# A fused attention block and gated network in float32: the weight sums of the second inner layer are formed and checked in the block runs, behind a third flag

## The chip, the core and the metric

One NeuronCore of a Trainium2 chip runs the whole program in one launch. Its engines are TensorE (PE, with the weight loads shown as PEld), VectorE (DVE), ScalarE (ACT) and GpSimd (POOL); SyncE (SP) issues all transfers, and its queue shows as SPq. The metric is the device time in microseconds.

## The reference

With `xn` the layer-normed input (2 batches of 2048 tokens, 256 channels), the output is `x + attn(xn) + ffn(xn)`, all in float32.

```python
def _L0_ffn_ref(x, w1_w, w1_s, w2_w, w2_s, h1_w, h1_s, h2_w, h2_s, w3_w, w3_s):
    h = silu(_tlin(x, w1_w, w1_s)) * _tlin(x, w2_w, w2_s)      # 256 -> 1024
    h = gelu(_tlin(h, h1_w, h1_s))                             # 1024 -> 1024, "first inner layer"
    h = gelu(_tlin(h, h2_w, h2_s))                             # 1024 -> 1024, "second inner layer"
    return _tlin(h, w3_w, w3_s)                                # 1024 -> 256
# _tlin(x, w, s) = einsum('bsi,oi->bso', x, w) * s, and the weights w are drawn from -1, 0, 1
```

`attn` is a linear attention block: convolutions over tokens, projections, q and k through elu, a 16-head product, a gate, an output projection, a third convolution, a norm and an MLP (256 to 1024 to 256 with gelu).

## The kernel before, in words

The 4096 tokens are 8 tiles of 512. Operands in float32 are split into a high part (type fp32r, whose low 12 bits are taken as zero) and the rest, so that a product is two or three fast matmuls. A weight of -1, 0 or 1 has nothing in its low part, so two matmuls do for the network. That this holds is not assumed: every weight piece, and every sum of pieces, is ORed with the mask 0xFFF into an accumulator (`check`), the accumulator is reduced (`bits`), summed over the partitions by a small matmul (`sum_bits`), written as a flag (`set_flag`), and TensorE loads the flag and branches to a variant of its program with wide or with fast matmuls.

**First half** (`P1_STEPS`): the attention's front, with the network's first layers for tiles 0 to 3 between. **Second half** (`E_STEPS`, -3 to 7): step i runs the output projection of tile i + 2, the MLP of tile i, the norm of tile i + 1 and the attention's rest of tile i + 3. These are the MLP's steps. In the text, step i begins with the output projection of tile i + 2; steps 6 and 7 have none and begin with fc1. Its order on VectorE: y_out(i - 1), x1_out(i + 2), the low parts of the gelus (`h_lo`, L1661) mixed with conv taps (L1424), moments (L1393), attention_out, add_lepe, checks, `pe_lo`, `pm_lo`, more checks. On GpSimd: halo, late sums (or, in step 0, at its end), inverse deviation, the gate (L922), `bias_residual` (L927). `pe_lo` and `pe_hi` are what the output projection of the next step reads.

**Block runs.** For the inner layers a tile is not multiplied by the whole weight directly: the 1024 x 1024 weight is cut into 2 x 2 quarters A11, A12, A21, A22 and the tile into B11 ... B22, and seven products (`PRODUCTS`) of sums of quarters take the place of eight. The weight sums S1 to S4 (`W_SUMS`) of both inner layers are formed on GpSimd, a slice of 128 rows at a time (`late_sums`, u = 0 to 7; u below 4 is the first inner layer, the others the second), in the MLP's steps: SP loads two pieces (`load_late`), GpSimd makes four sums of 128x512, VectorE checks the two halves of the result (and for the second inner layer the two raw pieces), SP saves them to DRAM (`save_sums`, s_s). Later SP loads each product's weights from w_s or s_s (`load_block`).

There are 12 runs of blocks. The first four, t = 0 to 3, each do the network's first layer for tile 4 + t (`first_layer`, on VectorE `gate_up`, on ScalarE `silu_gate`) and then the seven products of the first inner layer; the last eight do the second inner layer, one tile each, and the down projection (`down`). VectorE forms the inputs' sums (`combine`) and low parts (`low_part`, L1778) and adds the products (`sums_to_u2`, `sums_to_u4`, `result_22`, `result_12`, `result_21`). Each engine's order is written out by hand; everything is ordered by counting semaphores (`s_sum`: sums formed, `checked`: checks done, `bits_max`, `flag_set`, `prod`, `u_lo`), and all of an engine's waits are in program order, so an instruction behind a wait waits too. TensorE's second flag is set in step 7 and followed by the branch that holds all twelve runs (L2314 is the branch of the first flag, L2323 that of the second).

## Time and profile before

| | us |
|---|---|
| median of 3 runs | 1128.58 (1125.61 to 1132.94) |
| the profiled execution, whole | 1131.99 |
| its span in the trace | 1130.1 |
| busy: PE / PEld / DVE / ACT / POOL | 1043.5 (92%) / 920.2 (81%) / 769.4 (68%) / 592.7 (52%) / 279.8 (25%) |
| mean granted TensorE clock | 0.976 of full speed |

The profiled execution is one of its own, so a sum made from its rows is set against 1131.99 us, and then moved to the median. In its trace the steps of the second half that the change touches lie between about 425 and 682 us, the four runs with a first layer between 682 and 848, and the other eight behind.

### The profile page before, as it was taken

How to read it: one execution, taken by the hardware profiler on the slowest of the kernel's cores; microseconds unless marked ns; L12 is line 12 of the kernel's file. 1: busy time of each engine (PE TensorE's matmuls, PEld its weight loads, DVE VectorE, ACT ScalarE, POOL GpSimd, SP SyncE). 2: the span in 40 equal slices, each digit the busy share in tenths (PEclk: the TensorE clock that was granted, in tenths of full speed). 3: DMA queues.
4: the chain of work that ended last, by engine and by line, in shares of the span. 5: the costliest groups of instructions: out<-in, count | busy, mean ns of one | idle time of the engine just before them, and what ended most of it. 6: DMA issues, size and time to landing. Idle time of an engine off the chain costs nothing. (4 is left out here: it accounts for less than half of the span.)

```text
span 1130.1 us, 17148 instructions
## 1 busy us (share of the span) xinstructions
PE 1043.5 (92%) x6630; PEld 920.2 (81%) x6630; DVE 769.4 (68%) x948; ACT 592.7 (52%) x853; POOL 279.8 (25%) x231
## 2 busy tenths in 40 slices
PE   3579989999989999899998999999999999999998
PEld 2457877788867678577787878998999989999997
DVE  6586567644645647789988866466576888776764
ACT  3346776566634335444554544456456556554453
POOL 3144335331423323353444520000000110011100
PEclk9799989899999999899999999999999999999999
DMA  8767963554495455144443266121176322332310
GB/s 334 283 224 252 347 239 131 181 164 159 141 357 196 121 196 185 60 149 168 162 147 120 94 243 242 57 72 60 56 266 257 112 77 79 108 104 84 113 38 20
DMA packets 68339, 180.70 MB, mean 160 GB/s; under 512 B 4976, under 2 KB 26096, under 8 KB 64624
## 3 DMA queue, kind: packets, MB, share of 16 engines
q1 hardware_dynamic: 68256, 179.56, 45.7%
q8 instruction: 57, 0.93, 0.3%
q14 instruction: 26, 0.21, 0.1%
HBM read 121.86 MB, written 66.06 MB: 166 GB/s over the span
## 5 line engine op out<-in xcount | busy, mean ns | idle before, releaser
L2025 PE MATMUL pr<-xp_hi,wb 128*128 128x256 f32 x1344 | 320.0, 282 | 2.7 <-DVE p1s L1794 1.8
L2025 PE MATMUL pr<-xp_lo,wb 128*128 128x256 f32 x1344 | 319.5, 282 | 0.0
L2025 PEld LDWEIGHTS pr<-xp_hi,wb 128*128 128x128 f32 x1344 | 255.3, 190 | 4.6 <-issue 4.6
L2025 PEld LDWEIGHTS pr<-xp_lo,wb 128*128 128x128 f32 x1344 | 256.4, 191 | 0.0
L2025 PE MATMUL pr<-u_hi,ring 128*128 128x512 f32 x256 | 103.1, 403 | 2.3 <-issue 1.3
L2025 PE MATMUL pr<-u_lo,ring 128*128 128x512 f32 x256 | 100.7, 394 | 0.0
L983 POOL TENSOR_TENSOR ot<-ot,yg 128x512 f32<-128x512 f32 x14 | 25.2, 1802 | 277.0 <-DVE ot L1815 277.0
L1299 ACT CAST xp_hi<-tf 128x1024 fp32r<-128x1024 f32 x48 | 50.2, 1046 | 52.6 <-PE pr L2025 18.2
L2192 PE MATMUL pr<-wf_hi,h_hi 128*128 128x256 f32 x256 | 75.8, 296 | 0.0
L2192 PE MATMUL pr<-wf_lo,h_hi 128*128 128x256 f32 x256 | 73.0, 285 | 0.0
L2192 PE MATMUL pr<-wf_hi,h_lo 128*128 128x256 f32 x256 | 72.6, 284 | 0.0
L1778 DVE TENSOR_TENSOR xp_lo<-tf,xp_hi 128x1024 fp32r<-128x1024 f32 x48 | 59.1, 1231 | 19.9 <-ACT xp_hi L1299 19.8
L1239 ACT ACTIVATE hf<-pr,fb 128x512 f32<-128x512 f32 x64 | 44.1, 690 | 54.0 <-PE pr L190 40.1
L1661 DVE TENSOR_TENSOR h_lo<-hf,h_hi 128x512 fp32r<-128x512 f32 x64 | 51.7, 818 | 24.5 <-ACT h_hi L1239 24.5
L2025 PE MATMUL pr<-xg_hi,ring 128*128 128x512 f32 x128 | 54.4, 425 | 9.5 <-issue 4.9
L2025 PE MATMUL pr<-wd,a_hi 128*128 128x256 f32 x256 | 60.9, 281 | 2.1 <-DVE a_lo L1808 2.0
L2025 PEld LDWEIGHTS pr<-u_hi,ring 128*128 128x128 f32 x256 | 48.6, 190 | 15.5 <-issue 3.7
L2025 PE MATMUL pr<-wd,a_lo 128*128 128x256 f32 x256 | 60.5, 279 | 0.0
L869 POOL TENSOR_TENSOR u_lo<-full,u_hi 128x512 fp32r<-128x512 f32 x32 | 43.7, 1370 | 61.7 <-DVE u_hi L1531 61.7
L874 POOL TENSOR_TENSOR xg_lo<-xg_lo,xg_hi 128x1024 fp32r<-128x1024 f32 x8 | 20.6, 2574 | 155.2 <-ACT xg_hi L1095 155.2
L2025 PEld LDWEIGHTS pr<-u_lo,ring 128*128 128x128 f32 x256 | 48.6, 190 | 10.3 <-issue 0.5
L1315 ACT ACTIVATE u<-u,prm 128x256 f32<-128x256 f32 x96 | 41.0, 498 | 30.3 <-DVE u L1799 15.2
(219 smaller groups left out, 2623.9 us busy)
## 6 DMA issues: line engine op xcount, KB each, us to landing
ring<-w_s SPq DMA_DIRECT2D x42, 512.0 KB, 5.0
uf<-h_s SPq DMA_DIRECT2D x16, 1024.0 KB, 6.0
late_raw<-w_gated SPq DMA_DIRECT2D x16, 512.0 KB, 5.3
s_s<-late_sum SPq DMA_DIRECT2D x8, 1024.0 KB, 6.6
wb<-s_s SPq DMA_DIRECT2D x8, 1024.0 KB, 8.6
stage<-w_gated SPq DMA_DIRECT2D x4, 1536.0 KB, 10.5
wb<-w_s SPq DMA_DIRECT2D x6, 1024.0 KB, 10.2
vw<-v_s SPq DMA_DIRECT2D x8, 514.0 KB, 7.4
```

Source lines behind the costliest of these rows:

```text
L869: pool.tensor_tensor(u1_lo[:, m, :], full1[:, m % 2, :], u1_hi[:, m, :].bitcast(F32), ALU.subtract) \
L874: pool.tensor_tensor(x_lo[:], xf, x_hi[:].bitcast(F32), ALU.subtract).then_inc(s["x_split"], 1)
L983: pool.tensor_tensor(ot[:, part, :], ot[:, part, :], yg[:, part, :], ALU.add).then_inc(s["out_sum"], 1)
L1239: last = e.activation(out_, F1[:, m % 2, :], ACT.Gelu, bias=fb[:, m:m + 1])
L1299: e.copy(xp_hi[p][:], sources[p]).then_inc(s["u_hi"], 1)
L1315: last = e.activation(results[k][:, m, :], source[:, m, :], ACT.Gelu, scale=par(scale, RESULTS[k][0] * HB + m))
L1661: e.tensor_tensor(h_lo[:, m, :], hf[:, m % 2, :], h_hi[:, m, :].bitcast(F32), ALU.subtract) \
L1778: e.tensor_tensor(xp_lo[p][:], sources[p], xp_hi[p][:].bitcast(F32), ALU.subtract).then_inc(s["u_lo"], 1)
L2025: return e.matmul(bank, w.bitcast(dt), v_.bitcast(dt), start=first, stop=last, skip_group_check=True)
L2192: last = e.matmul(as_tokens(F2)[:, n, :], h[:, k, cols], w[:, k, :], start=(k == 0 and j == 0), stop=(k == KH - 1 and j == 2))
```

## The change

The second inner layer's sums (old u = 4 to 7) leave the MLP's steps. What stays there is spread over steps 1, 2, 4 and 5, one slice each with two checks; the two checks of the down weights go to steps 0 and 3, ahead of `pe_lo`; the bits are reduced in step 5. `bias_residual` moves on GpSimd from behind the gate to the head of the step, behind the halo and ahead of the sums.

In each of block runs 0 to 3, one slice of the second inner layer is now treated in a new buffer, late2, in the place where the down weights lie: SP loads two pieces, VectorE checks them behind gate_up 1 and 3 (into a new accumulator, acc3), GpSimd forms the four sums in place behind these two checks and the low part of xg, VectorE checks them ahead of sums_to_u2 and behind the last `low_part`, SP saves them. In run 3 the accumulator is reduced, and the bits are summed on TensorE ahead of the last product. The second flag now stands for the first inner layer and the down weights; the second branch holds runs 0 to 3, and a third flag with its own branch holds the other eight. On SP the down weights load behind the second layer's blocks, load_xg comes behind save_sums2 and save_result(t - 1, 3), and some loads around load_block(1, ...) change places. The matmuls are the same ones, and 16 checks of VectorE and 16 additions of GpSimd move from the steps to the runs; one reduction, one memset, two small sets of bit sums and one branch are added.

```diff
-LATE = tuple((layer, m) for layer in range(2) for m in range(HB))
-LATE_LOADS = {(0, "first"): (0, 1), (1, "first"): (2,), (2, "first"): (3,), (3, "first"): (4,), (4, "first"): (5,),
-              (5, "first"): (6,), (6, "first"): (7,)}
-LATE_SUMS = {(0, "last"): (0,), **{(i, "first"): (i,) for i in range(1, 8)}}
-LATE_CHECKS = {1: (0, 1), **{i: (i,) for i in range(2, 8)}}
-def checks_of(u):
-    return ["sums"] * 2 + ["raw"] * 2 * LATE[u][0]
+LATE_LOADS = {0: (0, 1), 3: (2,), 4: (3,)}
+LATE_SUMS = {1: 0, 2: 1, 4: 2, 5: 3}
+LAST_CHECKS = (0, 3)
+IN_PLACE = ("S2", "S4", "S3", "S1")
 def checks_before(u):
-    return 1 + sum(len(checks_of(n)) for n in range(u)) + (u >= 3)
+    return 1 + 2 * u + (u >= 2)
+LATE_CHECKS = 2 + 2 * HB
+RUN_CHECKS = 4
...
+        late2 = place("late2", [P, 2, PIECE], RG + 69632)
+        acc3 = place("acc3", [P, PIECE], wo_at, I32)
...
         def sums_kept(e):
             for i in range(2):
-                e.wait_ge(s_kept[i], s_kept_before[i] + 16 * HB)
+                e.wait_ge(s_kept[i], s_kept_before[i] + 16 * (HB // 2))
+        def sums2_kept(e, count):
+            e.wait_ge(s_kept[0], s_kept_before[0] + 16 * (HB // 2 + count))
...
+            def load_late2(n):
+                if n == 0:
+                    sp.wait_ge(s["bits_max"], 2)
+                else:
+                    sums2_kept(sp, n)
+                    sp.wait_ge(s["checked"], STREAM + 3 + LATE_CHECKS + RUN_CHECKS * n)
+                for i in range(2):
+                    sp.dma_start(late2[:, i, :], w_gated[KH // 2 + KH + n + i * HB]).then_inc(late_in[0], 16)
+            def save_sums2(n):
+                sp.wait_ge(s["s_sum"], len(W_SUMS) * (HB + n + 1))
+                sp.dma_start(s_s[HB + n], late2[:].rearrange("p a (b n) -> p (a b) n", b=2)).then_inc(s_kept[0], 16)
...
-                for place in ("first", "last"):
-                    for u in LATE_SUMS.get((i, place), ()):
-                        save_sums(u)
-                for u in LATE_LOADS.get((i, "last"), ()):
-                    load_late(u)
+                if i in LATE_SUMS:
+                    save_sums(LATE_SUMS[i])
                 if i == E_STEPS[-1]:
+                    load_late2(0)
                     load_block(0, 1)
                     load_block(0, 2)
...
             save_y(TILES - 1)
-            sp.wait_ge(s["bits_max"], 2)
-            for i in range(2):
-                sp.dma_start(wd_[:, i, :].bitcast(F32), w_s[STREAM + KH + i]).then_inc(s["wd_in"], 16)
             for t_ in range(BLOCK_RUNS - 1):
-                load_xg(FRONTED + t_ + 1, xg2)
                 if t_ > 0:
                     save_result(t_ - 1, 3)
+                save_sums2(t_)
+                load_xg(FRONTED + t_ + 1, xg2)
                 for k in range(3):
                     save_result(t_, k)
+                load_late2(t_ + 1)
+            save_sums2(BLOCK_RUNS - 1)
             load_block(1, 0)
+            load_block(1, 1)
             save_result(BLOCK_RUNS - 2, 3)
-            load_block(1, 1)
             load_h(0, 0)
+            load_h(0, 1)
             load_block(1, 2)
-            load_h(0, 1)
             for k in range(len(RESULTS)):
                 save_result(BLOCK_RUNS - 1, k)
                 load_block(1, 3 + k)
+            sp.wait_ge(s["bits_max"], 3)
+            for i in range(2):
+                sp.dma_start(wd_[:, i, :].bitcast(F32), w_s[STREAM + KH + i]).then_inc(s["wd_in"], 16)
...
+            def late_sums2(n):
+                pool.wait_ge(s["checked"], STREAM + 3 + LATE_CHECKS + RUN_CHECKS * n + 2)
+                a11, a12, a21, a22 = (late2[:, i // 2, i % 2 * TOK:(i % 2 + 1) * TOK] for i in range(4))
+                before = len(W_SUMS) * (HB + n)
+                pool.tensor_tensor(a22, a21, a22, ALU.add).then_inc(s["s_sum"], 1)
+                pool.tensor_tensor(a21, a11, a21, ALU.subtract).then_inc(s["s_sum"], 1)
+                pool.wait_ge(s["s_sum"], before + 1)
+                pool.tensor_tensor(a11, a22, a11, ALU.subtract).then_inc(s["s_sum"], 1)
+                pool.wait_ge(s["s_sum"], before + 3)
+                pool.tensor_tensor(a12, a12, a11, ALU.subtract).then_inc(s["s_sum"], 1)
...
+                if i >= 0 and valid(i + 2):
+                    bias_residual(i + 2)
                 if i == 0:
                     pool.wait_ge(s["h1_mm"], KH * FRONTED)
                     pool.wait_ge(s["checked"], STREAM + 1)
                     pool.memset(acc2[:], 0).then_inc(s["checked"], 1)
-                for u in LATE_SUMS.get((i, "first"), ()):
-                    late_sums(u)
+                if i in LATE_SUMS:
+                    late_sums(LATE_SUMS[i])
...
-                if valid(i + 1) and valid(i + 2):
-                    bias_residual(i + 2)
-                for u in LATE_SUMS.get((i, "last"), ()):
-                    late_sums(u)
+                if i == -1:
+                    bias_residual(1)
                 front("e", i, "after_back")
-            for j in range(FRONTED, TILES):
-                low_of_xg(j, xg2_lo, xg2, xg2_hi)
+            pool.wait_ge(s["g_prod"], TILES)
+            pool.wait_ge(s["checked"], STREAM + 2 + LATE_CHECKS)
+            pool.memset(acc3[:], 0).then_inc(s["checked"], 1)
+            for n in range(BLOCK_RUNS):
+                low_of_xg(FRONTED + n, xg2_lo, xg2, xg2_hi)
+                late_sums2(n)
...
+            def check_late(u, n):
+                e.wait_ge(s["s_sum"], len(W_SUMS) * (u + 1))
+                sums = late_sum[u % 2][:].rearrange("p (a b) n -> p a (b n)", a=2)
+                check(STREAM + 2 + checks_before(u) + n, sums[:, n, :], acc2)
+            def check_late2(t, n):
+                if n < 2:
+                    e.wait_ge(late_in[0], 16 + 32 * (HB // 2 + t + 1))
                 else:
-                    e.wait_ge(late_in[u % 2], 16 + 32 * (u // 2 + 1))
-                    source = late_raw[u % 2][:, n % 2, :]
-                check(STREAM + 2 + checks_before(u) + n, source, acc2)
+                    e.wait_ge(s["s_sum"], len(W_SUMS) * (HB + t + 1))
+                check(STREAM + 3 + LATE_CHECKS + RUN_CHECKS * t + n, late2[:, n % 2, :], acc3)
+            def sum_up_bits(n, of, checks):
+                e.wait_ge(s["checked"], checks)
+                e.tensor_reduce(bits[:, n:n + 1], of[:], AX_X, ALU.max).then_inc(s["bits_max"], 1)
...
-                checks = [(u, n, what) for u in LATE_CHECKS.get(i, ()) for n, what in enumerate(checks_of(u))]
-                for late in checks[:3]:
-                    check_late(*late)
+                if i in LATE_SUMS:
+                    for n in range(2):
+                        check_late(LATE_SUMS[i], n)
+                if i in LAST_CHECKS:
+                    n = LAST_CHECKS.index(i)
+                    e.wait_ge(s["wd_in"], 16 * (n + 1))
+                    check(STREAM + 2 + (0, checks_before(2) - 1)[n], last_raw[:], acc2)
+                if i == max(LATE_SUMS):
+                    sum_up_bits(1, acc2, STREAM + 2 + LATE_CHECKS)
...
-                for late in checks[3:]:
-                    check_late(*late)
-                if i in (0, 2):
-                    e.wait_ge(s["wd_in"], 16 if i == 0 else 32)
-                    check(STREAM + 2 + (0 if i == 0 else checks_before(3) - 1), last_raw[:], acc2)
-                if i == max(LATE_CHECKS):
-                    e.wait_ge(s["checked"], STREAM + 2 + checks_before(len(LATE)))
-                    e.tensor_reduce(bits[:, 1:2], acc2[:], AX_X, ALU.max).then_inc(s["bits_max"], 1)
...
+                    if m in (1, 3):
+                        check_late2(t_, m // 2)
...
+                check_late2(t_, 2)
                 sums_to_u2(t_)
                 sums_to_u4(t_)
                 low_part(t_, 5)
                 low_part(t_, 6)
+                check_late2(t_, 3)
+                if t_ + 1 == BLOCK_RUNS:
+                    sum_up_bits(2, acc3, STREAM + 3 + LATE_CHECKS + RUN_CHECKS * BLOCK_RUNS)
                 result_22(t_)
                 if t_ + 1 == BLOCK_RUNS:
+                    set_flag(2, pr[3][0:1, 0, 0:1])
                     combine(t_ + 1, 1)
                     low_part(t_ + 1, 0)
                 result_12(t_)
...
-            def gated_network(wide):
+            def first_runs(wide):
                 e.wait_ge(s["wf_in"], 48 + 16 * (KH // 2))
                 for t_ in range(BLOCK_RUNS):
                     first_layer(FRONTED + t_, wide)
                     for p in range(NP):
+                        if t_ + 1 == BLOCK_RUNS and p + 1 == NP:
+                            e.wait_ge(s["gated"], KH * TILES)
+                            sum_bits(2, pr[3][0:1, 0, 0:1])
                         product(t_, p, wide)
+            def last_runs(wide):
                 for r in range(TILES):
...
-            any_wide = e.value_load(wide_flag[0:1, 1:2])
+            more_wide = e.value_load(wide_flag[0:1, 1:2])
+            with e.If(more_wide > 0):
+                first_runs(True)
+            with e.Else():
+                first_runs(False)
+            e.wait_ge(s["flag_set"], 3)
+            any_wide = e.value_load(wide_flag[0:1, 2:3])
             with e.If(any_wide > 0):
-                gated_network(True)
+                last_runs(True)
             with e.Else():
-                gated_network(False)
+                last_runs(False)
```

## Rows read from the trace of the kernel before

**Rows 1.** Table by stretch (us), each engine's busy time, PEclk, DMA share, GB/s.

```profile
532.00:564.00 32.00, 30.37 (x177) 24.62 (x176) 29.61 (x36) 17.66 (x27) 14.42 (x10) 1.00 0.39 137
697.00:738.00 41.00, 40.92 (x288) 38.50 (x288) 24.31 (x25) 21.50 (x31) 2.40 (x1) 1.00 0.17 56
```

**Rows 2.** TensorE's waits, 425 to 700 us: us in total, times, longest.

```profile
PE pr L190 <- DVE pe_lo L1630: 7.7, 4, 2.5
PE pr L2128 <- DMA qa<-q_s: 2.8, 1, 2.8
PE pr L2020 <- DVE bits L1740: 1.9, 1, 1.9
...
PE pr L190 <- DVE pm_lo L1655: 0.8, 1, 0.8
```

**Rows 3.** Timeline of TensorE, heads of steps 5 and 6: start, us, operation [idle before].

```profile
596.97 0.50 PE L190 MATMUL pr<-pe_hi,wo_hi 128*128 128x512 f32 x1 [2.50 <-DVE pe_lo L1630]
...
627.66 0.50 PE L190 MATMUL pr<-pm_hi,wf_hi 128*128 128x512 f32 x1 [0.79 <-DVE pm_lo L1655]
```

**Rows 4.** Timeline of VectorE, steps 1, 3, 5 and 6.

```profile
476.66 1.41 DVE L1424 SCALAR_TENSOR_TENSOR conv<-vw,prm,conv 128x512 f32<-128x512 f32 x2
...
486.23 7.89 DVE L1454 SCALAR_TENSOR_TENSOR acc<-late_sum,acc 128x1024 int32<-128x1024 int32 x3
494.04 1.21 DVE L1630 TENSOR_TENSOR pe_lo<-acte,pe_hi 128x1024 fp32r<-128x1024 f32 x1
...
539.81 2.44 DVE L1424 SCALAR_TENSOR_TENSOR x<-x,prm,x 128x512 f32<-128x512 f32 x2
...
559.45 3.31 DVE L1630 TENSOR_TENSOR pe_lo<-acte,pe_hi 128x1024 fp32r<-128x1024 f32 x1
...
615.28 1.42 DVE L1393 BATCH_NORM_STATS2 st_h<-pr 128x6 f32<-128x256 f32 x4
...
641.91 1.42 DVE L1393 BATCH_NORM_STATS2 st_h<-pr 128x6 f32<-128x256 f32 x4
```

**Rows 5.** One line's instructions: ns min/median/max, first and last start.

```profile
L940 POOL TENSOR_TENSOR late_sum<-late_raw x8: 1262/1745/2349, 451.7 to 646.3; 128x512 f32<-128x512 f32 x8
...
L1636 DVE SCALAR_TENSOR_TENSOR x<-pr,prm,x x16: 735/742/755, 357.7 to 600.9; 128x512 f32<-128x512 f32 x16
```

**Rows 6.** Timeline of GpSimd, step 3, the bias beside `pe_lo`.

```profile
558.30 3.38 POOL L927 TENSOR_TENSOR y<-y,fc_bias 128x1024 f32<-128x1024 f32 x1
```

**Rows 7.** Table by stretch, head of step 2.

```profile
495.00:501.00 6.00, 5.69 (x18) 4.52 (x19) 4.82 (x6) 1.27 (x2) 0.00 (x0) 0.72 0.27 87
```

**Rows 8.** Loads from issue to landing: of last_raw, then of late_raw.

```profile
DMA to landing us min/median/max: 7.1/7.2/7.2
...
DMA to landing us min/median/max: 3.5/5.3/6.7
```

**Rows 9.** Chain that ended last, in order of time: start, us, what.

```profile
650.35 2.87 PE pr L2192 x24
...
676.27 4.48 PE pr L2192 x24
...
682.24 14.77 PE pr L2025 x64
...
738.49 41.33 PE pr L2025 x288
```

**Rows 10.** The branches of the first and the second flag, as Rows 5.

```profile
L2314 PEldq COMPARE_BRANCH  x1: 3871/3871/3871, 48.1 to 48.1; - x1
...
L2323 PEldq COMPARE_BRANCH  x1: 4290/4290/4290, 677.4 to 677.4; - x1
```

**Rows 11.** Timeline of TensorE, first matmul behind the first flag's branch.

```profile
52.12 0.77 PE L2025 MATMUL pr<-xg_hi,ring 128*128 128x512 f32 x1 [4.91 <-issue]
```

**Rows 12.** Timeline of VectorE, first layer of block run 1.

```profile
733.02 0.75 DVE L1754 SCALAR_TENSOR_TENSOR uf<-pr,prm,silu 128x512 f32<-128x512 f32 x1 [1.06 <-PE pr L2025]
...
735.50 1.22 DVE L1778 TENSOR_TENSOR xp_lo<-uf,xp_hi 128x1024 fp32r<-128x1024 f32 x1
```

More of the change, by code:

```diff
@@ L277, in program @@
         ones = keep("ones", [P, 1])
-        bits = keep("bits", [P, 2])
-        wide_flag = keep("wide_flag", [1, 2], I32)
+        bits = keep("bits", [P, 3])
+        wide_flag = keep("wide_flag", [1, 3], I32)
         assert small_at[0] <= 15360, small_at
@@ L604, in save_sums @@
                 sp.wait_ge(s["s_sum"], len(W_SUMS) * (u + 1))
-                sp.dma_start(s_s[HB * LATE[u][0] + LATE[u][1]], late_sum[u % 2][:]).then_inc(s_kept[u % 2], 16)
+                sp.dma_start(s_s[u], late_sum[u % 2][:]).then_inc(s_kept[u % 2], 16)
             def load_block(layer, p):
@@ L611, in load_block @@
                 if name in W_SUMS:
-                    sums_kept(sp)
-                    source = s_s[HB * layer:HB * (layer + 1), :, W_SUMS.index(name), :]
+                    if layer == 0:
+                        sums_kept(sp)
+                    else:
+                        sums2_kept(sp, HB)
+                    source = s_s[HB * layer:HB * (layer + 1), :, (W_SUMS, IN_PLACE)[layer].index(name), :]
                 else:
@@ L740, in _ @@
                     load_residual(i + YS - 1)
-                for u in LATE_LOADS.get((i, "first"), ()):
+                for u in LATE_LOADS.get(i, ()):
                     load_late(u)
@@ L1667, in y_out @@
                 e.tensor_tensor(y[:, i % YS], as_tokens(F2), y[:, i % YS], ALU.add).then_inc(s["i_y"], 1)
-            def check_late(u, n, what):
-                if what == "sums":
-                    e.wait_ge(s["s_sum"], len(W_SUMS) * (u + 1))
-                    source = late_sum[u % 2][:].rearrange("p (a b) n -> p a (b n)", a=2)[:, n % 2, :]
-                else:
-                    e.wait_ge(late_in[u % 2], 16 + 32 * (u // 2 + 1))
-                    source = late_raw[u % 2][:, n % 2, :]
-                check(STREAM + 2 + checks_before(u) + n, source, acc2)
+            def check_late(u, n):
[5 more added lines that the diff above has]
+                    e.wait_ge(late_in[0], 16 + 32 * (HB // 2 + t + 1))
+                else:
+                    e.wait_ge(s["s_sum"], len(W_SUMS) * (HB + t + 1))
[3 more added lines that the diff above has]
+                e.tensor_reduce(bits[:, n:n + 1], of[:], AX_X, ALU.max).then_inc(s["bits_max"], 1)
             denominators(0)
```

5 lines of the change are left out of this document (1 added, 4 removed).

## The prediction

> **What bounds the kernel now.** The page's averages (TensorE busy 92% of the span, VectorE 68%) hide the stages, so the first view is the table by stretch [rows 1]. MLP step 3 leaves TensorE 1.6 us idle and VectorE 2.4 us of 32; a block run leaves TensorE 0.1 us in 41 and VectorE 16.7 us. So work that leaves the steps can pay, and work put into the runs is free only while it hides behind TensorE.
>
> What TensorE waits for between 425 and 700 us is in the view of the waits [rows 2]: at the head of steps 2, 3, 4 and 5 the output projection waits for `pe_lo`, 7.7 us in four waits, the longest 2.5 [rows 2, 3]. `pe_lo` is the end of the chain add_lepe, gate (GpSimd), `pe_hi` (ScalarE), `pe_lo`. Two things stand in it [rows 4, 6]. Checks (`acc`) lie in VectorE's queue ahead of `pe_lo`, three of them in steps 1 and 4. And `bias_residual` follows the gate on GpSimd, and `pe_lo` takes 3.31 us beside it where it takes 1.21 without it.
>
> The reason is a price that the rest needs: VectorE operations with two SBUF inputs and GpSimd's large tensor_tensor don't run side by side, they take turns. A pair of conv taps takes 2.44 us beside one `late_sum` operation and 1.41 alone, and GpSimd's own 1.26 becomes 1.75 and 2.35 [rows 4, 5]. So each 128x512 GpSimd operation takes some 1.15 us from a VectorE that has such work (between 1.03, the taps' loss, and its own 1.26), and a 128x1024 one 2.1 us (3.31 - 1.21). Operations that read PSUM pay nothing: `x1_out` never took over 0.755 us [rows 5].
>
> **Steps 1 to 6.** (a) The tail gets shorter: the bias no longer meets `pe_lo` (2.1 us off in steps 1 to 4), and steps 1 and 4 have two checks ahead of `pe_lo` instead of three (1.1 us each). The four waits of 7.7 us and the 0.8 at the head of step 6 go: **8.5 us** [rows 2].
> (b) What is late next is the head of the step. There GpSimd now has the bias (2.1) ahead of the four sums (4 x 1.15 = 4.6) in steps 1, 2, 4 and 5, all against h_lo and the conv taps. Step 5 takes 15.5 us from the end of its 12 projection matmuls (596.97 + 2.8) to its moments at 615.28; step 6, with nothing on GpSimd there, 14.25 (627.66 to 641.91) [rows 3, 4]. So 4.6 us of GpSimd cost 1.2 there and 3.4 went into waits for ScalarE. That room is used up, and I take the next 2.1 us as carried whole, since VectorE has next to no gap from its first conv tap to the moments: 4 x 2.1 = **8.4 us lost**. In step 3 only the bias is left, which fits into the 3.4: **1.2 gained**. The bounds are 0 and 8.4 lost.
> (c) After the wait of 2.5 us ahead of step 2 the granted clock of TensorE was 0.72 from 495 to 501 [rows 7]: 0.28 x 6 = **1.7 us** lost. Without the wait I expect no dip; in the stretch that holds one of the shorter waits, 532 to 564, the clock stayed at 1.00 [rows 1].
> (d) Step 0: the check of the down weights moves ahead of `pe_lo`(3) and waits for its load, issued at 443.20 and landed 7.1 us later [rows 8]. `pe_lo`(3), `pm_lo`(1) and SP's load of `acte` queue behind it for some 3 us. Free: TensorE waits 2.8 us for the load of q there anyway [rows 2].
>
> Sum: 8.5 - 8.4 + 1.2 + 1.7 = 3.0 us. The extra checks that go from behind `pm_lo` in steps 1, 4, 5 and 6 are also VectorE time, but `x1_out` behind them waits for the projection, so I give them nothing.
>
> **Step 7.** Its four checks and the reduction go elsewhere; TensorE's wait of 1.9 us for `bits` ends, and the 24 fc2 matmuls after it took 4.48 us instead of 2.87, which is the lower clock [rows 2, 9]: 3.5 us. Part comes back. The branch on the flag began at 677.4, 1.4 us after the bit sums (676.03), while matmuls were still queued, and took 4.29 us, to 681.7; fc2 and y_out just hid it, the next matmul came at 682.24 [rows 10, 9]. Now fc2 (2.9) and y_out with what lies around it (682.24 - 680.75 = 1.5) end 4.4 us after the bit sums, and the branch ends at 5.1 (set flag 0.5, load 0.35, branch 4.2), since all 24 matmuls can be queued before. That leaves 3.5 - 0.7 = **2.8 us**. MLP side: 5.8 us gained.
>
> **Block runs.** Per run VectorE gets 4 checks (4 x 1.22 = 4.9 us) and is stopped by four GpSimd sums (4.6), against 16 us of idle. By place: gate_up comes every 1.81 us with 1.06 idle ahead of it [rows 12], so a check of 1.14 in that gap pushes the next by 0.1, and the bank has a full unit of room. The sums start behind the second check and meet combine 1 and `low_part` 0, 1 and combine 2. `low_part`(0) of run 1 ended at 736.7 and TensorE began product 0 at 738.49 [rows 12, 9]: 1.8 us of room. Two GpSimd operations lie ahead of it, of which 1.2 us land on it, and 0.6 is left. The two later checks fit the gaps of 1.2 and 2.6 us ahead of sums_to_u2 and result_22. SP: the next pair of pieces is issued behind save_result(t,2), at some 723.5 in run 0, and such a load lands 3.5 to 6.7 us later [rows 8]; the first check wants it at 728.3 and TensorE feels it from some 730.2, so only the slowest landing costs, 0.2 to 0.5. load_xg now stands behind save_sums2 and save_result(t-1,3), some 9 us later; its `x_split` has 7 us of room left. The last save_result(2,3) stands behind load_block(1,1), which waits for the last sums; sums_to_u2 of run 3 waits for that save and may be up to 1 us late. I take **0.5 us** for all runs, bounds 0 and 14 (the rival below). The down weights load later, at about 853, wanted at 871.
>
> **The third flag.** In run 3 the bit sums stand ahead of product 6, whose 32 matmuls cover 3.8 us (24 like them took 2.87) [rows 9]. The flag is set some 0.5 us behind them; VectorE waits there some 3 us behind result_22, with combine(4,1) and `low_part`(4,0) queued behind; run 4 starts later by the branch as well, and has VectorE idle to absorb the rest. The branch is the price: it took 3.87 and 4.29 us [rows 10]. If TensorE's sequencer runs ahead by the whole product, load and branch end 5.1 us after the bit sums and TensorE stands 1.1 us. At the second flag it was some 16 matmuls ahead (by 677.0, 8 of 24 at 0.12 us had run); if that is the limit, it reaches the load 1.5 us later and TensorE stands 2.6. With nothing ahead it is the 4.91 of the first flag [rows 11]. I take **1.3 us**; 16 is what was left to queue there, and nothing shows a limit.
>
> The Trainium skill (TensorE: Matmul & The Clock Gate, the table at its head) gives TensorE's queue a depth of 64 instructions, which would be all of product 6 with its weight loads; by that the stand is 1.1 us, by the sixteen of the trace 2.6. The 24 matmuls and 24 loads at the second flag agree, as far as they reach.
>
> **Sum** against the profiled execution's own 1131.99 us: -5.8 + 0.5 + 1.3 = -4.0. That execution lies 3.4 above the median of the runs, so against the median: 1128.6 - 4.0 = **1124.6 us**. One per cent is 11.3 us, about what a measurement can tell from no change.
>
> **Rivals.**
> *The bias at the head costs nothing* (0.15). For: before, 3.4 of 4.6 us were absorbed. Against: VectorE is gapless behind the first conv tap. Then all 8.4 come back: 1116 us.
> *GpSimd's sums stop VectorE in the runs* (0.10): place, combine 1 and `low_part`(0); if all four operations (4.6 us) and 0.7 of checks come ahead of it instead of 1.2 us, TensorE waits 5.3 - 1.8 = 3.5 us in each of four runs, 14 in all. It decides when more than 1.8 us stand ahead of `low_part`(0). Then 1124.6 + 13.5 = 1138 us, slower. For: the chain is gapless there. Against: the two engines alternate in every row seen.
> *The gaps at the branches* (0.20): flags 2 and 3 leave TensorE 2.1 and 2.6 to 4.9 us, and the clock drops after them as after 1.9 us at 676: 1.6 us each, 3.2 in all, and up to 3.6 more (4.9 instead of 1.3). 1124.6 + 3.2 to 6.8 = 1128 to 1131, no change.
> *It doesn't shorten the steps* (0.05): if something else sets `pe_lo`, such as the gate alone, only step 7 and the costs stay: 1128.
>
> **How the numbers follow.** My case holds 0.50. Range: from the first rival (1116, with 2 us of spread between runs: 1114) to the third and a little beyond (1134); the second rival's far end stays out. Below 1117.3: 0.12 of the first rival and 0.04 of my own case, with its spread, 0.16. Over 1139.9: 0.05. Between: 0.79.
>
> **What would show it.** No wait for `pe_lo` over 0.5 us in steps 2 to 5; moments of steps 1, 2, 4, 5 some 2 us later behind the projection and of step 3 earlier; 24 fc2 matmuls of step 7 in 2.9 us; a branch of about 4 us ahead of the first run's first matmul and a gap of 1 to 3 us between product 6 of run 3 and product 0 of run 4; 41.3 us per run otherwise. A run over 42 us, or a new wait on `xp_lo`, proves the second rival; a clock under 1 behind either flag the third.

## The result, and the profile after

The changed kernel takes **1137.34 us** (median of 9 runs, 1135.13 to 1140.07), the kernel before beside it 1132.67 (9 runs): ratio **1.0055 [1.0034, 1.0075]**. A second comparison gave 1.0061 [1.0037, 1.0085]. It is slower by 6 to 7 us; 4 us faster was forecast, and the range ended at 1134. The forecast started from 1128.58, the median of three runs of the kernel before; over nine runs that median is 4.1 us higher. One execution each of two experiments below (No third flag, The condition turned round) took about 1694 us at a granted clock near 0.56 and is left out of their ratios.

The profiled execution after took 1137.34 us with a span of 1135.3 us. Its table by stretch (columns as in [rows 1]) shows an MLP step, a block run, and three stretches around the third flag:

```profile
532.00:564.00 32.00, 31.52 (x184) 25.99 (x183) 23.77 (x35) 18.18 (x28) 8.34 (x7) 1.00 0.42 148
690.00:731.00 41.00, 41.00 (x287) 38.54 (x288) 30.51 (x28) 21.53 (x31) 9.72 (x6) 1.00 0.30 103
832.00:850.00 18.00, 13.37 (x102) 12.99 (x102) 14.99 (x14) 8.05 (x15) 0.00 (x0) 0.88 0.84 296
850.00:857.00 7.00, 6.50 (x34) 6.23 (x35) 2.36 (x2) 1.03 (x2) 0.00 (x0) 0.62 1.07 399
```

The first two rows answer to [rows 1]. The step's TensorE is busier (31.5 of 32 us, before 30.4). The block run now carries 30.5 us of VectorE and 9.7 of GpSimd (before 24.3 and 2.4), and TensorE has no gap in it. The other two rows are where the time went: 4.6 us of 18 without work, then a granted clock of 0.62.

TensorE's waits from 425 to 700 us, answering to [rows 2]:

```profile
PE pr L192 <- ACT h_hi L1280: 9.6, 10, 2.4
PE pr L2078 <- DVE y L1708: 1.9, 1, 1.9
PE pr L192 <- DVE zi L1647: 0.9, 1, 0.9
```

All four waits for `pe_lo` (7.7 us) and the one for `bits` (1.9) are gone. Ten waits for gelu's `h_hi` at the head of the steps stand in their place, 9.6 us (before: three, 1.4 us). The wait for the load of q (2.8 us) is missing too. And from 700 us on, where TensorE before waited for nothing of the kind:

```profile
PE pr L2078 <- ACT u L1356: 4.8, 1, 4.8
PE pr L2078 <- DVE u L1830: 3.2, 2, 2.5
```

Both lie in the fourth run and at its end. TensorE's timeline (start, us, operation, idle before) has them with the head of the first layer:

```profile
673.53 0.47 PE L2078 MATMUL pr<-xg_hi,wgu 128*128 128x512 f32 x1 [1.95 <-DVE y L1708]
...
831.92 0.55 PE L2078 MATMUL pr<-xp_hi,wb 128*128 128x256 f32 x1 [2.46 <-DVE u L1830]
850.12 0.55 PE L2078 MATMUL pr<-xp_hi,wb 128*128 128x256 f32 x1 [4.75 <-ACT u L1356]
855.53 0.39 PE L2078 MATMUL pr<-xp_hi,wb 128*128 128x256 f32 x1 [0.38 <-issue]
```

The line at 850.12 names ScalarE's `u`. The third flag's load and branch, in the views of those lines (ns min/median/max, first and last start), say otherwise; the branches of the first two flags stand above them, answering to [rows 10]:

```profile
L2372 PEldq COMPARE_BRANCH  x1: 3791/3791/3791, 47.8 to 47.8; - x1
...
L2381 PEldq COMPARE_BRANCH  x1: 3530/3530/3530, 669.7 to 669.7; - x1
...
L2386 PEldq TENSOR_LOAD <-wide_flag x1: 542/542/542, 843.1 to 843.1; - x1
...
L2387 PEldq COMPARE_BRANCH  x1: 6174/6174/6174, 843.7 to 843.7; - x1
```

The third branch took **6.17 us**, from 843.7 to 849.9, and the matmul came at 850.12. TensorE had run dry at 845.37 (850.12 - 4.75).

Cut at the same marks, the two profiles differ like this (us; the first matmul of the output projection of step 1, of the first layer, of product 0 in run 3, of product 0 in run 4; "again" is a second profile of the changed kernel):

| stretch | before | after | again |
|---|---|---|---|
| start to step 1 | 458.5 | 453.6 | 453.1 |
| steps 1 to 7 | 223.75 | 219.98 | 219.69 |
| first layer to run 3 | 138.97 | 140.66 | 139.14 |
| run 3 up to run 4 | 26.63 | 35.93 | 36.18 |
| run 4 to the end | 282.3 | 285.2 | 285.0 |

The first row isn't clear. The profiles of the experiments that share the changed kernel's first half had 452.7 to 458.1 us there; the kernel before had 458.5. The wait for q's load doesn't order them: the profile with 452.7 had 2.3 us of it, the one with 458.1 none. So part of the 4.9 us is chance, and part may be the change's. Without that row the two profiles of the changed kernel stand 10.1 and 8.4 us behind, with it 5.2 and 3.0; the ratios say 6 to 7. What repeats in these two is this: **4 us gained in steps 1 to 7, 12 lost from run 3 on**.

The gain of steps 1 to 7 has to be read with the clock. Seven profiles have the changed kernel's steps; they took 219.6 to 220.1 us in five, 217.5 and 216.2 in the others (The save first, Quiet transfers). The difference lies for the most part in stretches in which the granted clock was at its lower level, 1.2 GHz. Steps 1 to 6 (to the first matmul of step 7's fc1) of the kernel before, of the changed one, and of the profile with 216.2:

```profile
458.49:653.17 194.68, 183.35 (x1053) 150.60 (x1053) 174.94 (x206) 97.40 (x151) 86.36 (x60) 0.98 0.36 128
453.55:647.50 193.95, 183.45 (x1053) 151.43 (x1053) 155.97 (x194) 97.59 (x151) 62.32 (x49) 0.97 0.26 90
454.72:644.80 190.08, 179.07 (x1053) 147.86 (x1053) 155.56 (x194) 97.42 (x151) 62.36 (x49) 1.00 0.27 92
```

So steps 1 to 6 of the changed kernel gained only 0.7 us; the other 3.0 of the 3.8 are step 7's.

### The profile page after: what moved, and what is told of

It reads as the page before. It is cut to its first block, busy times and chain, and to the rows that moved or that the text cites. A ratio compares the mean times of both kernels' runs of the same rounds, so it can differ in the third digit from the quotient of the medians.

```text
span 1135.3 us, 17164 instructions
## 1 busy us (share of the span) xinstructions
PE 1048.4 (92%) x6636; PEld 925.7 (82%) x6636; DVE 766.5 (68%) x950; ACT 592.6 (52%) x853; POOL 281.5 (25%) x232
## 4 chain that ended last, share of the span: by engine, by line
PE 70%; DVE 12%; ACT 5%; issue 5%; DMA 4%; POOL 2%; SPq 0%; DVEq 0%; ACTq 0%; POOLq 0%
PE pr L2078 43%; PE pr L192 12%; PE pr L2245 8%; DVE x L1465 3%; DVE h_lo L1702 2%; PE pr L178 2%; PE pr L185 2%; PE pr L2056 1%; DMA xn_s<-xh 1%; PE pr L2200 1%; DVE acc L1495 1%; ACT u L1356 1%; DMA h_s<-p1s 1%; ACT h_hi L1280 1%; DVE st_a L1434 1%
## 5 line engine op out<-in xcount | busy, mean ns | idle before, releaser
L2078 PE MATMUL pr<-xp_hi,wb 128*128 128x256 f32 x1344 | 323.9, 284 | 10.1 <-ACT u L1356 4.8
L2078 PE MATMUL pr<-xp_lo,wb 128*128 128x256 f32 x1344 | 322.8, 283 | 0.0
L1824 DVE TENSOR_TENSOR xp_lo<-tf,xp_hi 128x1024 fp32r<-128x1024 f32 x48 | 60.8, 1267 | 24.3 <-ACT xp_hi L1340 24.2
L1702 DVE TENSOR_TENSOR h_lo<-hf,h_hi 128x512 fp32r<-128x512 f32 x64 | 59.8, 953 | 23.6 <-ACT h_hi L1280 23.6
L192 PE MATMUL pr<-pm_hi,wf_hi 128*128 128x512 f32 x128 | 53.5, 418 | 10.9 <-ACT h_hi L1280 9.6
## 6 DMA issues: line engine op xcount, KB each, us to landing
wb<-w_s SPq DMA_DIRECT2D x6, 1024.0 KB, 10.1
```

The source lines that it names most:

```text
L192: last = e.matmul(out, w(k), v(k), start=(k == 0 and n == 0), stop=(k == chunks - 1 and n == 2))
L1702: e.tensor_tensor(h_lo[:, m, :], hf[:, m % 2, :], h_hi[:, m, :].bitcast(F32), ALU.subtract) \
L1824: e.tensor_tensor(xp_lo[p][:], sources[p], xp_hi[p][:].bitcast(F32), ALU.subtract).then_inc(s["u_lo"], 1)
L2078: return e.matmul(bank, w.bitcast(dt), v_.bitcast(dt), start=first, stop=last, skip_group_check=True)
```

## The experiments

All ratios are to the kernel before on the same chip, with 95% intervals; each edit is against the changed kernel unless it says so.

**The changed kernel again**, no edit.

> The changed kernel once more, unaltered, as the common mark for the three kernels beside it. Both theories: 1.002 to 1.009 of the kernel before. If the wait for the projected queries that vanished from step 0 (4.9 us of the profiles' difference) is the change's work, it is absent here too; if it was chance of the transfers, it may come back, and the profile is then 3 to 5 us longer up to the first of steps 1 to 7.

Measured 1.0061 [1.0037, 1.0085]. The steps and the losses are the same to 0.3 us (table above); the wait for q is absent.

**The save first.**

```
             load_block(1, 0)
-            load_block(1, 1)
             save_result(BLOCK_RUNS - 2, 3)
+            load_block(1, 1)
```

> One edit: the transfer of the third run's last result is issued ahead of the load of the second layer's second block, as in the kernel before, and not behind it. Theory (order of SyncE's queue): the transfer lands in about 3.6 us in place of 6.3, the sums of the fourth run aren't held up, TensorE's wait of 2.46 us in that run is gone and the kernel is 2 to 3 us faster than the changed one; with nothing else it stands at about 1.003 of the kernel before. Rival (the 0.5 MB have to move in any case, and VectorE's added checks make the fourth run's sums late by themselves): no change of more than 0.5 us, the wait stays with another releaser.

Measured 1.0022 [1.0001, 1.0042], 4.4 us better than the changed kernel. In the changed kernel's queue (timeline of SyncE) the save is issued 2.2 us behind the load, and VectorE's first sum of run 3 waits for its landing:

```profile
821.93 0.37 SPq L643 DMA_DIRECT2D wb<-s_s  x1
824.12 0.36 SPq L648 DMA_DIRECT2D h_s<-u  x1
```

```profile
830.55 1.23 DVE L1830 TENSOR_TENSOR u<-pr,p1s 128x1024 f32<-128x1024 f32 x1 [3.12 <-DMA h_s<-u]
```

It landed 6.3 us after its issue. With the save first:

```profile
820.71 0.37 SPq L648 DMA_DIRECT2D h_s<-u  x1
821.18 0.45 SPq L643 DMA_DIRECT2D wb<-s_s  x1
```

```profile
824.41 1.23 DVE L1830 TENSOR_TENSOR u<-pr,p1s 128x1024 f32<-128x1024 f32 x1 [0.39 <-DMA h_s<-u]
```

It lands after 3.6 us, TensorE's wait is gone and run 3 takes 31.9 us (changed 35.9). The save is issued as long after the start of run 3 as before (9.8 us, changed 9.9), so the whole effect is in its landing. The theory of the queue's order stands. By the profiles 2 to 3 us was too small; the ratios alone, with their intervals, don't tell 4.4 from it. The next kernel, without the third branch, shows the wait and the stretch behind it by themselves:

```profile
835.26 0.36 PE L2077 MATMUL pr<-xp_hi,wb 128*128 128x256 f32 x1 [2.27 <-DVE u L1830]
```

```profile
835.00:846.00 11.00, 10.74 (x77) 10.78 (x78) 9.35 (x9) 3.59 (x6) 0.00 (x0) 0.84 0.68 221
846.00:852.00 6.00, 6.00 (x53) 6.00 (x53) 5.85 (x6) 4.10 (x9) 0.00 (x0) 1.00 1.07 400
```

A wait of 2.27 us and 0.16 x 11 = 1.8 us of clock make 4.1; that kernel's run 3 took 30.6 us against 26.6 before. The clock's part doesn't always come: of the seven profiles with this wait five had it, and two had not, after waits of 2.99 (A near target) and 2.74 us (The bias behind the gate). The first of them:

```profile
835.00:846.00 11.00, 11.00 (x97) 10.83 (x96) 9.55 (x10) 5.40 (x10) 0.00 (x0) 1.00 0.98 332
```

**No third flag.**

```
-                    set_flag(2, pr[3][0:1, 0, 0:1])
...
-                        if t_ + 1 == BLOCK_RUNS and p + 1 == NP:
-                            e.wait_ge(s["gated"], KH * TILES)
-                            sum_bits(2, pr[3][0:1, 0, 0:1])
...
-            e.wait_ge(s["flag_set"], 3)
-            any_wide = e.value_load(wide_flag[0:1, 2:3])
-            with e.If(any_wide > 0):
-                last_runs(True)
-            with e.Else():
-                last_runs(False)
+            last_runs(False)
```

> Left out: the third flag, its sum over partitions, and TensorE's branch on it; the last eight runs are there in their fast form only. The checks and their reduction stay. Theory (the third branch is the largest part of the loss): TensorE goes from product 27 to product 28 without a gap, the 4.75 us of idle time, the 0.4 us behind it and the slow matmuls (about 2.4 us) go, 7 to 8 us in all: 0.998 to 1.000 of the kernel before. Rival (the branch covers a wait that would be there anyway, for the next block's low parts or its load): under 3 us gained, with a wait for VectorE or a transfer at product 28.

Measured 0.9988 [0.9972, 1.0003], 8.2 us better (1.0061 - 0.9988 of 1130; the two intervals leave some 3 us either way). In the profile of the changed kernel the gap of 4.75 us and run 4, 35.2 us there against 32.2 before, make 7.8. Product 28 follows without a gap. So the branch hid nothing else: the named `u` was ready.

**The condition turned round.**

```
-            with e.If(any_wide > 0):
-                last_runs(True)
+            with e.If(any_wide < 1):
+                last_runs(False)
             with e.Else():
-                last_runs(False)
+                last_runs(True)
```

> One edit: the condition of the third branch is turned round, so that the fast form of the last eight runs follows the branch directly and the exact form lies behind it. Theory (what is paid is the fetch of instructions at a far target, behind the data transfers that fill the queues there): the branch takes under 1 us in place of 6.2, no idle time, 5 to 8 us faster than the changed kernel. Rival (the price is the branch itself, the sequencer starting afresh whichever way it goes): the branch takes 3.5 to 6.2 us as before and the time is that of the changed kernel within 1 us.

Measured 0.9999 [0.9980, 1.0018], 7.0 us better with the flag, its sum and its load all kept. The third branch:

```profile
L2387 PEldq COMPARE_BRANCH  x2: 73/1918/3764, 842.0 to 1120.2; - x2
```

The branch that falls through took **73 ns**, at 842.0. The second instruction of the line, 3.76 us at 1120.2, is the jump over the other arm at the end, where TensorE has finished. The flag, its sum and its load show no price beyond this jump and the noise (0.9999 against 0.9988 without them); the price is in going to the other arm.

**A near target.**

```
             with e.If(any_wide > 0):
-                last_runs(True)
-            with e.Else():
-                last_runs(False)
+                product(BLOCK_RUNS, 0, True)
+            last_runs(False)
```

> One edit: of the exact form of the last eight runs only its first product stands in the arm that the third branch passes over (the rest of that arm, never executed here, is left out), so that the branch is taken as before, but its target lies 64 instructions on and not some thousands. Theory D (distance: the target was not yet fetched): the branch takes under 1 us, no idle time, 1.000 of the kernel before like the turned condition. Theory T (a taken branch makes the sequencer fetch afresh, however near its target): 3.3 to 6.4 us as before and the time of the changed kernel, 1.005 to 1.007.

Measured 1.0000 [0.9975, 1.0024], and the branch, taken as before:

```profile
L2387 PEldq COMPARE_BRANCH  x1: 225/225/225, 842.3 to 842.3; - x1
```

Theory D holds: a taken branch is cheap when its target lies 64 instructions on (32 matmuls and their weight loads), and takes microseconds when it lies behind the whole other form of eight runs. This kernel does not have the exact form of the last eight runs, so it serves for the time alone.

**Quiet transfers.**

```
             load_h(0, 1)
+            sp.wait_ge(s["prod"], NP * BLOCK_RUNS + 1)
             load_block(1, 2)
```

> One edit: SyncE holds back the loads of the second layer's third and later blocks until TensorE has done the product behind the third branch, so that few or no data transfers run while it is taken. Theory (the fetch at the target waits behind data in the transfer engines: at the first two branches, with idle queues, it took 3.3 to 3.9 us, at the third 6.1 to 6.4): the third branch takes 3.3 to 3.9 us here. Rival (this branch is dearer by what it jumps over or to): 6 us again. The time of the kernel is of no weight here: blocks come late, and TensorE will wait 5 to 15 us for them later.

The far branch and the stretch in which it ran, first here and then in the changed kernel (table by stretch; DMA share and GB/s are the last two columns):

```profile
L2388 PEldq COMPARE_BRANCH  x1: 3686/3686/3686, 839.8 to 839.8; - x1
...
839.00:844.00 5.00, 2.97 (x25) 2.80 (x24) 5.00 (x6) 3.12 (x6) 0.00 (x0) 1.00 0.02 3
```

```profile
841.00:850.00 9.00, 4.37 (x40) 4.08 (x38) 8.21 (x8) 5.91 (x11) 0.00 (x0) 0.92 1.04 385
```

The same branch over the same distance took 3.69 us at 3 GB/s and 6.05, 6.17, 6.37 and 6.45 us in the four profiles with data all around it. The difference, some 2.5 us, comes with the data. The expectation calls the queues at the first two branches idle; in the changed kernel the transfers ran at 126 GB/s during the first and at 13 during the second.

The view of the transfers shows what the branch waits for. Beside the data it has a queue q8 of the kind "instruction", with 59 packets and 0.97 MB in the whole program, so 16 KB each. In every profile each far branch has just one such packet inside; it is read here as the instructions at the target. In the changed kernel the branch runs from 843.68 to 849.85; of the stretches 843.68 to 847.4 and 847.4 to 847.7 the first has data only, the second has the packet:

```profile
q1 hardware_dynamic: 1010, 1.49, 106.5%
...
q8 instruction: 1, 0.02, 20.1%
```

With quiet transfers the branch begins at 839.76. From there to 840.6 nothing moves, and from 840.6 to 841 the packet is all that does:

```profile
DMA packets 0, 0.00 MB, mean 0 GB/s; under 512 B 0, under 2 KB 0, under 8 KB 0
...
q8 instruction: 1, 0.02, 21.5%
```

So the packet starts some 3.8 us into the branch with the transfers full, and 1.0 us into it with them quiet, and takes 1.0 and 1.4 us itself (20.1% and 21.5% of 16 engines' time in stretches of 0.3 and 0.4 us). The whole difference is the time before it starts. During the branch that falls through and the one to the near target there is no such packet, nor in the 2 us behind them. The kernel as a whole took 1.0094 [1.0065, 1.0122], since the blocks came late, as meant.

**The bias behind the gate again.**

```
-                if i >= 0 and valid(i + 2):
-                    bias_residual(i + 2)
...
-                if i == -1:
-                    bias_residual(1)
+                if valid(i + 1) and valid(i + 2):
+                    bias_residual(i + 2)
```

> One edit to the changed kernel: GpSimd adds the bias to the residual behind the gate again, at the end of a step, and not at its head; the sums and checks stay where the change put them. Theory (the head of a step pays for the bias and the sums: the ten waits for gelu, 9.6 us, are made by ScalarE and VectorE being held there): about half of the 9.6 us go, but the waits for the low part of the gated attention at the end of the step come back in part (1.2 us each as worked out for the tails): 0 to 3 us faster than the changed kernel. Rival (GpSimd at the tail holds VectorE as before): waits of 7 us for pe_lo come back whole and the kernel is 2 to 4 us slower than the changed one.

Measured 0.9993 [0.9974, 1.0012], 7.7 us better than the changed kernel, more than either theory gave. Its steps 1 to 7 took 212.1 us (changed 219.98, before 223.75), and TensorE's waits from 425 to 700 us were:

```profile
PE pr L192 <- DVE pe_lo L1669: 3.0, 3, 1.4
PE pr L192 <- ACT h_hi L1278: 1.9, 2, 1.1
```

The groups of VectorE's `h_lo` between 450 and 670 us (count, busy us, mean ns, then idle before) say what the bias at the head does; first the changed kernel (its second profile), then this one:

```profile
L1702 DVE TENSOR_TENSOR h_lo<-hf,h_hi 128x512 fp32r<-128x512 f32 x56 | 53.1, 967 | 21.2 <-ACT h_hi L1280 21.2
```

```profile
L1700 DVE TENSOR_TENSOR h_lo<-hf,h_hi 128x512 fp32r<-128x512 f32 x56 | 42.8, 772 | 24.5 <-ACT h_hi L1278 24.5
```

The 56 `h_lo` cost 10.3 us more when the bias stands ahead of the sums on GpSimd, since more of GpSimd's work then falls on them. Part of the 7.8 us of steps 1 to 7 is the clock: at its lower level it cost 5.1 us there in the changed kernel (three stretches of 1.7) and 1.7 in this one.

**The bias alone**, in the kernel before.

```
                     halo(i + 2, x1, "g_x1", 1, "x1_halo")
+                if i >= 0 and valid(i + 2):
+                    bias_residual(i + 2)
...
-                if valid(i + 1) and valid(i + 2):
-                    bias_residual(i + 2)
+                if i == -1:
+                    bias_residual(1)
```

> The kernel before with the one edit that the bias is added at the head of a step. It is the change without its moved sums, its checks and its third flag. Theory (what shortened steps 1 to 7 by 3.8 us is that late work left the tail of a step, the bias first of all): 2 to 4 us faster than the kernel before, 0.9965 to 0.998, with pe_lo's 7.7 us of waits gone or halved, and waits for gelu at the head. Rival (it was the checks of the second layer that left, so that bias alone only moves the wait from tail to head): within 1 us of the kernel before.

Measured 1.0028 [1.0013, 1.0043]: **slower** by 3 us. Both theories fall on the time, though the waits moved as the first one said.

```profile
PE pr L190 <- ACT h_hi L1241: 11.3, 12, 2.4
...
PE pr L190 <- DVE pe_lo L1632: 0.5, 1, 0.5
```

The waits for `pe_lo` fell from 7.7 us to 0.5 and those for `h_hi` rose from 1.4 to 11.3. Steps 1 to 7 took 226.45 us, 2.7 more than before.

**Three repairs together:** the save first, the bias behind the gate, the condition of the third branch turned round (the edits shown above).

> The changed kernel with three edits together: the bias behind the gate again, the third run's last result transferred ahead of the block load, the condition of the third branch turned round. Moved sums, checks and third flag stay. Theory (the three losses lie in different places and add up): by the ratios of the single edits to the changed kernel (0.9932, 0.9961, 0.9939 of 1.006) it stands at 0.987 to 0.992 of the kernel before, 9 to 14 us faster. Rival (what one edit frees, another wait takes: VectorE's checks and ScalarE's gelu hold the fourth run and the first layer): 0.993 to 0.997.

Measured 1119.46 us, **0.9903 [0.9867, 0.9938]**. The product of the single ratios is 0.989. Run 3 took 27.0 us.

**The branches of the kernel before laid out anew.**

```
             some_wide = e.value_load(wide_flag[0:1, 0:1])
-            with e.If(some_wide > 0):
-                first_half(True)
-                second_half(E_STEPS[0:3], True)
-            with e.Else():
-                first_half(False)
-                second_half(E_STEPS[0:3], False)
-            second_half(E_STEPS[3:], False)
...
+            with e.If(some_wide < 1):
+                first_half(False)
+                second_half(E_STEPS[0:3], False)
+                second_half(E_STEPS[3:], False)
+                e.wait_ge(s["flag_set"], 2)
+                any_wide = e.value_load(wide_flag[0:1, 1:2])
+                with e.If(any_wide < 1):
+                    gated_network(False)
+                with e.Else():
+                    gated_network(True)
+            with e.Else():
...
```

> The kernel before, with its two branches laid out so that the fast form follows each directly, nested, without a jump behind it. Theory (a taken branch to a far target costs its fetch, 3.9 and 4.3 us, less what TensorE still has queued): TensorE's gap of 4.91 us behind the first branch falls to about 1 us, and the second gives back 1 us or less, since y is awaited there; 3.5 to 5 us faster, 0.9955 to 0.997. Rival (behind the first branch the gap is VectorE's and the ring's, the branch lies beside it): 1 us or less.

Measured 0.9940 [0.9918, 0.9963], 6.8 us, somewhat more than forecast. The matmul behind the first flag, answering to [rows 11]:

```profile
48.26 0.47 PE L2025 MATMUL pr<-xg_hi,ring 128*128 128x512 f32 x1 [1.15 <-DVE wide_flag L1467]
```

The gap fell from 4.91 us to 1.15. The second branch gave back only 0.3 us (steps 1 to 7: 223.42), since `y` is awaited there. At the end the jump over the other arm costs something: from the last matmul to the end of the span it is 6.0 us (1122.4 - 1116.4), before 4.4 (1130.1 - 1125.7). Of the 6.8 us, 3.8 + 0.3 - 1.6 = 2.5 are traced so; the rest lies ahead of step 1, where this profile is 9.4 us earlier than the one of before, 5.6 more than the gap, with a granted clock of 0.97 against 0.96 up to there, and where profiles of one code differ by as much (452.7 to 458.1).

**All of it together:** the three repairs, and all three branches nested like this.

> The kernel e9_repaired with all three branches laid out as in the one beside it (nested, the fast form behind each). Theory: the gains of the two kernels add, 13 to 18 us under the kernel before, 0.984 to 0.989; no branch takes over 0.3 us. Rival (the first half is bound by its transfers, so that an earlier start is given back in it): the time of e9_repaired within 1 us.

Measured **1111.09 us** (1109.90 to 1114.12), **0.9840 [0.981, 0.987]**: faster than both kernels. The three branches:

```profile
L2370 PEldq COMPARE_BRANCH  x1: 95/95/95, 47.7 to 47.7; - x1
...
L2376 PEldq COMPARE_BRANCH  x1: 73/73/73, 654.0 to 654.0; - x1
...
L2380 PEldq COMPARE_BRANCH  x2: 65/1771/3477, 822.0 to 1100.6; - x2
```

## Why the prediction was wrong, point by point

**Where it held.** The steps got shorter, by 3.8 and 4.1 us where 5.8 were forecast. The waits for `pe_lo` went (8.5 us forecast, 7.7 and the 0.8 at the head of step 6 gone), the head of the step paid (8.4 forecast, the waits for `h_hi` rose by 8.2), and the third flag left a gap. The runs carry the moved work free: 41.4 us per run, and VectorE's low parts took up to 1.66 us beside GpSimd's sums without TensorE feeling it. The second rival fell. Step 7 gave 3.0 us (29.1 to 26.0), forecast 2.8.

**The step that failed most is the third flag: "I take 1.3 us".** It measured 8.2 us by ratios and 7.8 in the trace. Three terms were mis-sized:
- The branch. I took its length as about 4 us from the two rows of before [rows 10]. At those two the transfers ran at 150 and 192 GB/s (48 to 52 and 677 to 682 us); at the third they ran at 385, and it took 6.2. I had read the durations but not what ran beside them. The 2.5 us more are the time that the branch's instruction packet waits before it starts (Quiet transfers).
- How much TensorE has queued. I let all 32 matmuls of product 6 cover the branch. The load was issued at 843.1 and TensorE ran dry at 845.37: 2.3 us, the last 17 matmuls. This is the sixteen that I had read at the second flag and set aside with "nothing shows a limit". By it the gap is 0.6 (load to branch) + 6.17 + 0.3 (branch to matmul) - 2.3 = 4.8 us; measured 4.75. The Trainium skill (TensorE: Matmul & The Clock Gate, the table at its head) gives the queue 64 instructions, which would have been all of product 6; here the flag had been set at 841.5 and the sequencer reached the load only at 843.1. The trace disagrees, and the measurement decides. The second flag doesn't agree with 64 either, as the prediction says it does: in the kernel before, that flag was set at 676.45, and the load came at 677.04, with 17 of the 24 matmuls left.
- The clock. 850 to 857 went by at 0.62: 0.38 x 7 = 2.7 us. It was in the third rival with 1.6 us, and that rival, at 0.20 and up to 1131, was the nearest in its mechanism. It lacked the longer branch. In number the second rival's 1138 is nearer, but that is luck: the wait for `low_part` that it rests on didn't come.

**"sums_to_u2 of run 3 ... may be up to 1 us late"** and 0.5 us for all runs: measured a wait of 2.3 to 3.0 us and, in most profiles, 1.7 or 1.8 of clock; 4.1 in all in the profile without the third branch, 4.4 by the ratios. I had seen the place and the order in the queue, and priced the issue alone, which came no later; what came later is the landing, 6.3 us instead of 3.6 behind the 1 MB load. The clock's part was there in five of seven profiles.

**"Without the wait I expect no dip", 1.7 us gained.** Steps 1 to 6 were to gain 3.0 us and gained 0.7. The waits at tail and head came out about as put; the clock did not: in steps 1 to 6 of the kernel before it was at its lower level from the start of step 1 to 462 us and once more from 496.5 (3.7 us of loss), and in the changed kernel in three stretches:

```profile
472.00:477.00 5.00, 5.00 (x19) 3.46 (x17) 5.00 (x10) 3.33 (x5) 0.00 (x0) 0.66 0.71 213
506.00:511.00 5.00, 4.81 (x16) 3.66 (x17) 5.00 (x10) 3.38 (x6) 0.00 (x0) 0.66 0.71 221
605.00:610.00 5.00, 4.13 (x16) 3.51 (x17) 2.71 (x6) 3.26 (x6) 0.00 (x0) 0.66 0.32 129
```

That is 0.34 x 5 = 1.7 us each, 5.1 in all: 1.4 more than before, where 1.7 less was forecast. The same steps with the clock at 1.00 throughout (Quiet transfers) took 3.9 us less. Why the stretches come in one profile and not in another, no run shows.

**"The tail gets shorter: the bias no longer meets `pe_lo`", 8.5 us, against 8.4 at the head.** The sizes nearly cancel, as put, but the split hid what the change's own parts do. With the bias in its old place the moved sums and checks shorten steps 1 to 7 by 11.6 us (223.75 to 212.1); the bias at the head takes back 7.8 of them, and by itself costs the kernel before 2.7. Of the 11.6 us some 3.7 are clock, of the 7.8 some 3.4. The bias did free the tail, as credited (7.7 us of waits fell to 0.5 with it alone), but it paid more at the head than it freed; and I gave the extra checks "nothing", where with the sums they are the whole gain of the steps. With the bias behind the gate three waits of 3.0 us in all are left at `pe_lo`, so the moved sums and checks alone end 4.7 of the 7.7. Sums and checks were not moved one without the other, so how much is whose is not shown.

**The cold first layer** (16.4 us at 0.90 in the first profile of the changed kernel, 14.8 in the second) wasn't forecast. It came in three profiles, where TensorE's gap ahead of it was 1.95, 1.98 and 2.19 us, and not in six, with gaps of 1.61 to 1.81 in five and 2.01 in one.

**What stays open:** what makes profiles differ by up to 5 us ahead of step 1, and how much of that the change does; and what decides when q's load lands in step 0. No run tells it apart: the wait was 2.8, 2.6 and 1.7 us in three profiles with the old steps, and 0 to 0.5 in nine of ten with the new.

## What to carry to other kernels

Lay the arm that is always taken directly behind its branch, nested, so that no jump stands ahead of work; here a taken branch over the other form of the runs took 3.3 to 6.5 us, most with the transfers full, and what TensorE had queued, 17 matmuls, covered 2.3. When you price a gap of 2 to 3 us of TensorE, give the slow stretch behind it a chance of its own (here, ahead of the first layer, in run 3 and behind the third branch, it came with eight of twelve such gaps, at some 1.7 us), and price a transfer also by the bytes ahead of it, not only by when it is issued. Before you read a few microseconds out of two profiles, set the granted clock of the stretch beside them. When a change is made of several moves, do each alone: here the moved sums and checks were worth 11.6 us and the bias took 7.8 back.

## What the runs showed of the hardware

- The same compare-and-branch took 65 to 95 ns when it fell through, 225 ns to a target 64 instructions on, 3.3 to 4.4 us to a far target with transfers of 3 to 192 GB/s around it, and 6.0 to 6.5 us to a far target at 385 to 400 GB/s. Each far branch has one 16 KB packet of the kind "instruction" inside; it starts 0.9 to 1.9 us into the branch in the first group and 3.7 to 4.1 us into it in the second. What sets the length of that delay isn't shown: the second branch of the kernel before had transfers at 393 GB/s for its first 1.6 us, and its packet started between 1.6 and 2.1 us into it.
- TensorE's wait of 2.27 us was followed by 1.8 us of loss in clock, and the one of 4.75 us by 2.7; after one of 2.99 us the clock stayed at 1.00.
- When TensorE's sequencer issued the load of a flag, 17 matmuls with their weight loads were still to run, at the second flag and at the third (nothing was queued at the first), though the flag had been set 0.6 and 1.5 us before.
- The profile names the last releaser that it knows. For the gap of 4.75 us it named ScalarE's `u`; with the branch gone the gap was gone, so idle time that a branch makes can be put down to another engine.
